# A graph network on one core: transposed one-hots kept in DRAM, registers loaded a group ahead, gather and sum apart

## What is computed

```python
# message block, three times
msg = silu([h[src], h[dst], edge_attr] @ W1e + b1e) @ W2e + b2e
agg = segment_sum(msg, dst) / max(deg, 1)
h = h + silu([h, agg] @ W1n + b1n) @ W2n + b2n
# relation block, three layers, relu after the first two
seg = edge_type * n + dst
agg = segment_sum(x[src], seg) / max(count(seg), 1)
x = x @ root + b + sum_r agg[r] @ W[r]
```

## Time and profile before

| what | value |
|---|---|
| runs | 6395.67, 6398.9, 6404.14 us |
| the profiled execution, its own time | 6410.94 us |
| its span, first to last instruction | 6409.2 us |
| granted TensorE clock, mean | 0.94 of full speed |
| TensorE matmuls busy | 5167.9 us (81%) |
| TensorE weight loads busy | 4403.8 us (69%) |
| VectorE busy | 4519.1 us (71%) |
| GpSimd busy | 3388.0 us (53%) |
| ScalarE busy | 2721.7 us (42%) |
| DMA | 639.85 MB, 100 GB/s over the span |

### The profile page before, as it was taken

How to read it: one execution, slowest core, us unless ns; L and a number is a source line. 1 busy time by engine, 2 the same in 40 slices (tenths; PEclk the granted TensorE clock), 3 DMA queues, 4 the chain that set the end, 5 groups by cost and what they waited for, 6 DMA issues and landing times.

```text
span 6409.2 us, 169000 instructions
## 1 busy us (share of the span) xinstructions
PE 5167.9 (81%) x47647; PEld 4403.8 (69%) x47651; DVE 4519.1 (71%) x10320; ACT 2721.7 (42%) x4966; POOL 3388.0 (53%) x4176
## 2 busy tenths in 40 slices
PE   3666666614888888888898888999889989899898
PEld 2444444414777767777677776888878888788887
DVE  6444444413777767767667776999969999699996
ACT  1111111124666655555555554444434444344443
POOL 1777777722555535555355553555535555355552
PEclk9999997557999999999999999999989999899997
DMA  8111111167655546555455552112211112111120
GB/s 301 29 29 29 29 29 29 29 185 208 170 168 169 170 120 169 164 165 169 121 156 168 167 168 80 57 56 57 56 34 56 57 56 57 33 57 56 56 57 26
DMA packets 376130, 639.85 MB, mean 100 GB/s; under 512 B 68352, under 2 KB 80980, under 8 KB 376075
## 3 DMA queue, kind: packets, MB, share of 16 engines
q1 hardware_dynamic: 335016, 610.44, 31.6%
q0 software_dynamic: 38400, 28.13, 2.5%
q10 hardware_dynamic: 2658, 0.51, 0.0%
HBM read 564.82 MB, written 73.22 MB: 100 GB/s over the span
## 4 chain that ended last, share of the span: by engine, by line
PE 62%; POOL 17%; issue 10%; DMA 4%; ACT 3%; another core or an unknown queue 2%; DVE 2%; POOLq 0%; SPq 0%; ACTq 0%; DVEq 0%
PE sums L870 18%; PE sums L884 15%; POOL recs L489 13%; PE gat L845 11%; PE gat L847 10%; PE gat L850 4%; POOL arena L502 3%; ACT arena L641 3%; DMA arena<-recs 2%; DMA recs<-arena 1%; PE gat L950 1%; PE gat L948 1%; PE sums L961 0%; DVE arena L1103 0%
## 5 line engine op out<-in xcount | busy, mean ns | idle before, releaser
L845 PE MATMUL gat<-table,arena 128*128 x7680 | 1918.5, 250 | 277.9 <-ACT arena L641 164.2
L502 POOL TENSOR_SCALAR arena<-iota_f,arena 128x128 f32<-128x128 f32 x1920 | 1268.5, 676 | 1315.0 <-PE sums L884 1129.1
L847 PE MATMUL gat<-table,arena 128*128 x7680 | 1924.2, 251 | 0.0
L870 PE MATMUL sums<-arena 128*128 128x192 bf16 x15360 | 1887.7, 246 | 2.0 <-DVE arena L1245 2.0
L1245 DVE TENSOR_SCALAR arena<-iota_s,meta_t 128x512 bf16<-128x512 int16 x3840 | 1531.9, 471 | 111.8 <-PE sums L870 111.8
L870 PEld LDWEIGHTS sums<-arena 128*128 128x128 bf16 x15360 | 1325.9, 98 | 2.6 <-DVE arena L1245 2.6
L641 ACT CAST arena<-gat 128x768 bf16<-128x768 f32 x960 | 767.2, 799 | 1128.1 <-PE gat L847 1128.1
L1209 DVE TENSOR_SCALAR arena<-arena,lane 128x1024 bf16<-128x1024 bf16 x1920 | 1058.1, 592 | 192.3 <-DMA arena<-rows_d 191.4
L489 POOL DMA_INDIRECT recs<-arena x800 | 950.4, 1188 | 381.0 <-issue 378.6
L884 PE MATMUL sums<-arena 128*128 128x64 f32 (+1 forms) x7680 | 959.6, 278 | 207.5 <-issue 142.2
L884 PEld LDWEIGHTS sums<-arena 128*128 128x128 f32 x7680 | 898.6, 192 | 309.7 <-issue 309.5
(11 more groups left out here) (181 smaller groups left out, 4799.9 us busy)
## 6 DMA issues: line engine op xcount, KB each, us to landing
arena<-rows_d SPq DMA_DIRECT2D x480, 512.0 KB, 4.5
arena<-recs SPq DMA_DIRECT2D x640, 272.0 KB, 2.8
arena<-rows_d SPq DMA_DIRECT2D x480, 256.0 KB, 3.3
recs<-arena SPq DMA_DIRECT2D x1, 43520.0 KB, 122.6
recs<-arena POOLq DMA_INDIRECT x800, 2.9
arena<-in_edge_attr_dram SPq DMA_DIRECT2D x100, 62.5 KB
xn<-in_x_dram SPq DMA_DIRECT2D x1, 768.0 KB
out_dram<-nodes SPq DMA_DIRECT2D x1, 768.0 KB
```

The costliest lines, as they stand in the source:

```text
L502: ins = pool.tensor_scalar(oh[u % 2][:, j, :], iota_f[:], rec_in[u][:, j, PLACE:PLACE + 1], None, ALU.is_equal)
L845: pe.matmul(at, ohT[s][:, 0, j * P:(j + 1) * P], table_flat[:, bass.ds(off[j], K3)], start=True, stop=False)
L847: ins = pe.matmul(at, ohT[s][:, 1, j * P:(j + 1) * P], table_next[:, bass.ds(off[j], K3)], start=False, stop=l >= LAYERS)
L870: ins = pe.matmul(accp[s][:, 256 * r:256 * r + K3], oh4[s][:, t, r * P:(r + 1) * P], gb[u % 4][:, t, :], start=t == 0, stop=t == GT - 1)
```

## The change

1. **Transposed one-hots are made once.** Only the first message layer makes them, all three for every group. SyncE stores each group's (768 KB) to a new DRAM tensor `hots_d`. The five other layers load them from there: 768 KB a group in the message layers 1 and 2, 512 KB in the relation layers. `ohT` has four buffers; the spread rows, needed in the first layer alone, have two. The records are loaded as before.
2. **Registers are loaded a group ahead.** TensorE has two sets of registers. Those of the next group are loaded inside the present one: in the message layers after the first tile of the sums, in the relation layers after the fourth tile.
3. **Message layers gather a whole group, then sum** the group two before (before the change: the group one before). The gather waits for `gat_read` half by half instead of `z_ready` for the whole; VectorE adds the three parts half by half, six adds of 256 columns instead of two of 256 and two of 512, and frees each half of `gat` by itself.
4. **Relation layers:** the order of gather and sums stays; the waits of the sums move behind the gather of the first tile; the type one-hots have four buffers instead of two.

The diff, cut to its core:

```diff
+    hots_d = nc.dram_tensor("hots_d", [NG, P, 3 * GT * P], BF16, kind="Internal").ap()
...
         for s in range(4):
+            t, at = carve(at, 3 * GT * P // 2, BF16)
+            ohT.append(t.rearrange("p (m e) -> p m e", m=3))
+        rows_at = at
+        for s in range(2):
             t, at = carve(at, GT * P, BF16)
             row_in.append(t.rearrange("p (m e) -> p m e", m=2))
...
-        PRE = 4
+        PRE = 8
...
+            def load_rows(k, u):
+                sp.wait_ge(ohT_made, done(k - 2))
...
+            def load_records(l, k, u):
+                n = l * NG + k
+                sp.wait_ge(gat_read, done(2 * (n - 4) + 1))
...
+            def store_hots(k, u):
+                sp.wait_ge(ohT_made, done(k))
+                sp.sem_inc(hots_go, 1)
+                sp.dma_start(hots_by_group[:, bass.ds(k, 1), :].rearrange("p a w -> p (a w)"),
+                             ohT[u].rearrange("p m e -> p (m e)")).then_inc(hots_stored[u], 16)
+
+            def load_hots(l, k, u):
+                m = 3 if l < LAYERS else 2
+                sp.wait_ge(gathered, done(2 * (l * NG + k - 4) + 1))
+                sp.sem_inc(hots_go, 1)
+                sp.dma_start(ohT[u][:, 0:m, :].rearrange("p m e -> p (m e)"),
+                             hots_by_group[:, bass.ds(k, 1), 0:m * GT * P].rearrange("p a w -> p (a w)")
+                             ).then_inc(hots_loaded[u], 16)
...
+            with sp.Fori(1, QUADS) as i:
+                for u in range(4):
+                    load_rows(4 * i + u, u)
+                    load_records(0, 4 * i + u, u)
+                    store_hots(4 * i + u - 2, (u + 2) % 4)
...
+            for l in range(1, 2 * LAYERS):
                 with sp.Fori(0, QUADS) as i:
                     for u in range(4):
+                        load_hots(l, 4 * i + u, u)
                         if l < LAYERS:
+                            load_records(l, 4 * i + u, u)
...
+                def load_gather(g, u, l=l):
+
+                    pe.load(tile_regs[u % 2], offsets[0:1, bass.ds(GT * g, GT)])
+                    if l < LAYERS:
+                        pe.load([dst_reg[u % 2]], goff[0:1, bass.ds(3 * g, 1)])
+
+                def load_sums(g, u, l=l):
+
+                    if l < LAYERS:
+                        pe.load([sum_reg[u % 2]], goff[0:1, bass.ds(3 * g + 1, 1)])
...
+                def gather_tile(g, u, j, off, dst_off, l=l):
                     n = l * NG + g
+                    if j % 4 == 0:
+                        pe.wait_ge(gat_read, done(2 * (n - 1) + j // 4))
...
+                def stage(g, u, i, l=l):
...
+                    if l < LAYERS:
                         for j in range(GT):
+                            if gathers:
+                                gather_tile(g, u, j, off, dst_off)
+                        for j in range(GT):
+                            if adds:
+                                if j == 0:
+                                    sums_ready(g - 2, (u + 2) % 4)
+                                sums_tile(g - 2, (u + 2) % 4, j, to)
+                            if j == 0:
+                                next_places()
+                    else:
+                        for j in range(GT):
+                            if gathers:
+                                gather_tile(g, u, j, off, dst_off)
+                            if adds:
+                                if j == 0:
+                                    sums_ready(g - 2, (u + 2) % 4)
+                                sums_tile(g - 2, (u + 2) % 4, j, to)
+                            if j == 3:
+                                next_places()
...
                     for h in range(2):
                         tiles = slice(4 * h, 4 * h + 4)
                         dve.wait_ge(gathered, done(2 * n + h))
                         dve.tensor_tensor(z[s][:, tiles, :], parts[:, tiles, 0:HID], rec[:, tiles, 0:HID], ALU.add
                                           ).then_inc(z_step, 1)
-                    for k in range(1, 3):
-                        dve.wait_ge(z_step, 3 * n + 1 + k)
-                        ins = dve.tensor_tensor(z[s], z[s], parts[:, :, k * HID:(k + 1) * HID], ALU.add)
...
+                        dve.wait_ge(z_step, 4 * n + 2 * h + 2)
+                        ins = dve.tensor_tensor(z[s][:, tiles, :], z[s][:, tiles, :], parts[:, tiles, 2 * HID:K3],
+                                                ALU.add)
+                        ins.then_inc(gat_read, 1)
...
                 def type_hots(g, u, l=l):
                     n = l * NG + g
-                    s = u % 2
-                    dve.wait_ge(summed, done(n - 2))
+                    dve.wait_ge(summed, done(n - 4))
```

More of the change, by code:

```diff
@@ L912, in _ @@
+                load_gather(0, 0)
+                for g in range(4):
+                    stage(g, g, 0)
+                with pe.Fori(1, QUADS) as i:
+                    for u in range(4):
+                        stage(4 * i + u, u, i)
+                for g in range(NG, NG + 2):
+                    stage(g, g % 4, QUADS)
                 if l < LAYERS:
@@ L1137, in _ @@
             dve.wait_ge(rec_made, EG)
-            for q in (ohT_made, z_ready):
+            for q in (ohT_made, types_made):
                 dve.sem_inc(q, PRE)
+            for q in hots_stored:
+                dve.sem_inc(q, 16)
             def split_terms(l):
```

300 lines of the change are left out of this document (143 added, 157 removed).

## The result

The changed kernel takes 6187.3 us (median of 4 runs, 6182.1 to 6192.7), the kernel before took 6397.3 us beside it (4 runs, 6393.2 to 6404.1). The ratio is 0.967, 95% interval 0.9654 to 0.9688. The prediction said 6141 us, so the direction and the size hold, and 46 us of the gain are missing. The profiled execution took 6186.7 us, with a span of 6184.7 us.

What follows compares the result with a forecast made beforehand. VectorE was taken to bound the relation layers, TensorE's sequencer the message layers. 6410.9 - 307 - 6 + 26 + 29 = 6153 us, less 12 for the median: 6141 us, range 6050 to 6280, chance 0.80.

Steps and rivals of the forecast that it cites:

- Relation layers, - 307 predicted: Relation layers: without the transposed one-hots on VectorE, a group falls from 4.62 to 3.98 us, over 480 groups 307 us.
- a third collision with a GpSimd addition: Relation layers: all three GpSimd additions would delay VectorE's type one-hots by 0.55 us each, making 3.75 us a group.
- Layers 1 and 2, + 26 predicted: Message layers 1 and 2: TensorE's sequencer keeps every step and gains one, 4.66 to 4.74 us a group, over 320 groups.
- The added step: Message layers' gather: a second wait, for the second half of the PSUM tile, costs the sequencer about 0.09 us.
- they were not what ended last: Message layers: the looser order of waits saves nothing, since the sequencer's own work, not those waits, ended last.
- Layer 0, + 29 predicted: First message layer: the sequencer's 4.76 us a group becomes 4.94 us with two added waits, over 160 groups.
- The DMA's side: First message layer: rows and records 2.67 us plus the store 2.16 us, 4.83 us a group, just under the sequencer.
- That two row buffers suffice: First message layer: rows are needed 8 us after being asked for, against 4.5 us to landing plus a 2.2 us store.
- Layer starts, - 6 predicted: Starts of the three relation layers: the gather no longer waits for hots, saving 2 us each.
- Rival A: Message layers: register loads cost the sequencer nothing, TensorE limits layers 1 and 2 at some 4.05 us; 5846 us, chance 0.08.
- Rival B: Relation layers: no one-hot runs during GpSimd additions, so VectorE stays the limit at 4.5 us a group; 6390 us, chance 0.07.
- Rival C: First message layer: mixed reads and writes hold the DMA at 168 GB/s, 9.46 us a group; 6864 us, chance 0.05.

Runs made afterwards that it cites:

- f_old_work: Changed kernel, but in the relation layers VectorE again does its two old comparisons a group, into memory nobody reads: 6383.3 us, ratio 0.9967.
- g_load_at_start: Changed kernel with registers not loaded ahead: each group's loads stand at the start of its own stage, the sum's just before the sums; 6207.6 us.
- e_twelve: Changed kernel with one load of twelve registers for three in message layers, each group's places twelve words, starting at multiples of 16 bytes: 5919.2 us.
- h_one_back: Changed kernel, but message layers sum the group one back, as before the change, instead of two back: 6260.7 us, ratio 0.9768.
- a_store_third: Changed kernel with layer 0 storing 256 KB of hots a group instead of 768 KB, leaving two thirds of the one-hots out: 6120.2 us.
- i_twelve_ahead: e_twelve, but layer 0 loads the next group's registers at the start of a group's stage, ahead of its gather: 5849.7 us, ratio 0.9137.
- c_amid_gather: Changed kernel, but layer 0 loads the next registers after the gather's fourth tile instead of after the first sums matmul: 6339.5 us, ratio 0.9899.

## Why the prediction was right, and where it was off

**Relation layers, - 307 predicted, - 320 measured: right, and for the reason given.** VectorE was the limit, f_old_work brings it back as one; the next bound was named as TensorE at 3.94 us, and it is 3.948 us with TensorE busy 630.0 of 630 us. Of the 107 us a layer, the old VectorE work alone is worth 59 (f_old_work against the changed kernel, 686.8 - 627.8), the loads ahead 22 (g_load_at_start). If the two add up, 26 remain that were not isolated; the gather's wait for hots from the same VectorE queue is gone too, and no kernel put it back. One term in this step was mis-sized without harm: VectorE was put at 3.75 us a group, counting a third collision with a GpSimd addition at 0.55 us. It is 502.4 us in 630 (a busy share of 80%, where 85 to 90% was to show it), with 3.948 us a group 3.15 us, the 3.16 that the comparisons left. Where VectorE is never idle the estimate is nearer: in f_old_work the one-hots take 564.1 us in 680, with 4.32 us a group 3.58 us, while the comparisons fell from 0.71 us each to 0.49. This fits a collision that moved over to the one-hots there and not in the changed kernel, where VectorE waits for TensorE; no run isolates it.

**Layers 1 and 2, + 26 predicted, - 9 measured: the mechanism right, the small term wrong.** The message group was said to be the sequencer's sum of steps, unmoved by where the steps stand. e_twelve shows it by taking steps away. The added step (the second PSUM wait, 0.09 us) is in the sequencer's row, yet the group did not grow. It is of the size of what g_load_at_start (- 0.04 us) and h_one_back (+ 0.09 and + 0.01 us) move. One candidate for what offset it is in the old trace: in 700 us of layer 1 (2400 to 3100) TensorE's sums waited there 15.9 us for GpSimd's one-hots and 2.7 us for ScalarE's, 0.13 us a group, and in the changed kernel not at all.

```profile
PE sums L884 <- POOL arena L502: 15.9, 35, 0.5
```

So the looser order did take something away, against "they were not what ended last". But h_one_back tightens the order again without bringing these waits back, so the cause stays open. The pause of TensorE in the sums was said to be about 1.5 us; it is 0.77.

**Layer 0, + 29 predicted, + 97 measured: the step that failed.** It was "the sequencer's 4.76 us of now becomes 4.76 + 0.08 + 0.1 = 4.94 us", which took every sequencer step over at its duration from a trace without stores. Where the steps keep their durations the sum comes out (a_store_third, 4.944 us), in part by luck: its 0.08 us for the second wait did not show in layers 1 and 2, and layer 0 there ran at the 1.2 GHz level for 52 us, against 7 us before, which the sum does not hold. In the changed kernel the eight-register load takes 0.98 us instead of 0.595, + 62 us. The remaining 7 of the 97 us were not isolated; the 1.2 GHz level lasted 154 us there, the granted clock was 0.91 instead of 0.97. The prediction asked of the new traffic only whether the DMA would hold it; it did not ask whether a register load, which reads SBUF too, keeps its duration in that traffic.

The DMA's side was well sized: 4.83 us a group for the full DMA was the estimate, and i_twelve_ahead, where the DMA is full (0.98), runs at 4.70 us. That two row buffers suffice held in the changed kernel (1.6 us of waits for rows) and no longer in i_twelve_ahead, where rows take 7.5 us to land instead of the 4.5 + 2.2 of the sum.

**Layer starts, - 6 predicted, + 7.5 measured.** The trace shows layer 0 beginning 5.6 us earlier, and 13 us more from layer end to layer start over the five borders and the end. The 6 us that relation layers were to win at their starts did not come: the borders ahead of them changed by + 2.5, + 2.0 and - 0.4 us. Message layers now end with two groups of sums after the last gather instead of one, which fits the + 4 to + 5 us at two of the borders; it was not tried by itself.

**Rival A** (loads free for the sequencer, 5846 us) fell: the sequencer's steps still follow each other, and TensorE has a pause that ends with the third load. The Trainium skill, "Advanced Engine Details and Errata", Sequencer Loop, was cited with the caution that it would not shorten the sequencer's sum, and the trace agrees: matmuls already queued run while a load lasts (to 3604.52 above), no further step does.

**Rival B** (VectorE stays the limit, 6390 us) fell: 3.948 us. The Trainium skill, "SBUF — State Buffer", Who interferes with whom, calls the port pair of VectorE and GpSimd an exclusive lock; that the type one-hots last 472 ns in the mean against 345 ns alone agrees with some waiting at the additions. Their 3.15 us a group exclude the form that the rival took, in which none could run beside 2.4 us of additions.

**Rival C** (layer 0 held by the DMA at 168 GB/s, 6864 us) fell: 294 GB/s here, 339 GB/s in i_twelve_ahead. Its premise, that no stretch of the old trace mixes loads and stores, was right only for heavy traffic: the building of the records stores and loads at 28 to 30 GB/s. The price of mixing fell on TensorE's register loads more than on the transfers.

## What to carry to other kernels

When an engine with dynamic addresses is never full and its pauses end in "issue", add up its sequencer's steps; register loads were here worth merging and aligning before anything was reordered. A cost that is taken over from a trace holds for the traffic of that trace: when a change adds stores from SBUF, ask whether the register loads of those microseconds keep their length. Such a stage can answer to a moved instruction in either direction (the same edit cost 170 us in one kernel and gave 60 in its neighbour), so measure it again after every other change.

## What was not expected of the hardware

- A register load on TensorE's sequencer costs by address and number, not by number alone: one register 0.305 us; from a multiple of 16 bytes of the table eight 0.59 us, twelve 0.85 us, but ten 1.08 us; from 8 bytes off that grid eight 1.95 us and ten 2.41 us. These fit 0.29 us for each piece of 16 bytes and about 0.48 us for each piece of 8, if a load from off the grid is made of pieces of 8 alone; that is arithmetic on six values, not a mechanism shown.
- The eight-register load was slowed in the layer whose DMA traffic stores from SBUF while row broadcasts and records load into it: 0.98 us in the mean and up to 2.1 us at a share of 0.90, 0.605 us with a third of the stores, 0.595 us in a layer at a share of 0.81 without any store. With stores it can be as low as 0.63 us at 0.96 (g_load_at_start) and as high as 1.58 us at 0.82 (c_amid_gather). Which meeting of transfers does it stays open: in the trace of the changed kernel the loads that begin 0.5 to 1 us after a store's first packets average about 0.75 us, those 4.5 to 6 us after them 1.2 us (29 of them), but no run isolated that.
- Layer 0's DMA moved 339 GB/s at a share of 0.98 with broadcasts, loads and stores mixed in one queue, against the 363 GB/s of the plain fill before.
